# The routed experts' gate and up products, turned round: 32-place units and pieces of up to 384 tokens in place of tiles of 128 with the tokens standing

## The reference, cut to what matters

```python
xn = layernorm(x)                       # x: 8 x 1024 tokens of 512
s = recurrence(xn, W1, b1, W2, b2, init_h)       # gated scan over each sequence
# feed-forward part, T = 8192 tokens, E = 32 experts, H = 512, I = 1024
shared_out = (silu(xn @ sgw) * (xn @ suw)) @ sdw
topk_ids = argmax(xn @ gate_w)          # one expert for each token
xs = xn * sigmoid(max(xn @ gate_w))
g = grouped(xs sorted by expert, routed_gate_w)  # 512 -> 1024
u = grouped(xs sorted by expert, routed_up_w)    # 512 -> 1024
d = grouped(silu(g) * u, routed_down_w)          # 1024 -> 512
out = x + s * silu(shared_out + d in the tokens' order)
```

## Time and profile before

| | before |
|---|---|
| median of 3 runs | 4076.29 us (4075.59 to 4077.69) |
| the profiled execution's own time | 4077.65 us |
| its span in the trace | 4076.0 us |
| PE busy | 3984.7 us, 98% of the span |
| DVE busy, ACT busy | 1983.8 us (49%), 2003.6 us (49%) |
| POOL busy | 834.1 us (20%) |
| granted TensorE clock, mean | 0.991 |

### The profile page before, as it was taken

How to read it: one execution, slowest core, us unless ns; L and a number is a source line. 1 busy time by engine, 2 the same in 40 slices (tenths; PEclk the granted TensorE clock), 3 DMA queues, 4 the chain that set the end, 5 groups by cost and what they waited for, 6 DMA issues and landing times. The chain is left out here.

```text
span 4076.0 us, 51548 instructions
## 1 busy us (share of the span) xinstructions
PE 3984.7 (98%) x17849; PEld 3230.3 (79%) x17852; DVE 1983.8 (49%) x2711; ACT 2003.6 (49%) x2512; POOL 834.1 (20%) x927
## 2 busy tenths in 40 slices
PE   7999999999989999999999999799999999999998
PEld 6888888888867888888888888588888888888886
DVE  4232323233345555555555555455656556565564
ACT  3222222222247766766676666454545455554552
POOL 2011110101014100000000000043434434444443
PEclk9999999999989999999999999899999999999999
DMA  4122121212121000110000010455657557566562
GB/s 164 65 78 77 74 80 72 82 51 90 44 81 44 32 32 31 51 42 31 31 31 31 34 59 10 151 196 190 213 173 255 196 190 258 200 229 216 191 229 87
DMA packets 197850, 447.44 MB, mean 110 GB/s; under 512 B 19737, under 2 KB 36313, under 8 KB 193954
## 3 DMA queue, kind: packets, MB, share of 16 engines
q1 hardware_dynamic: 165170, 346.24, 24.0%
q0 software_dynamic: 32624, 100.47, 7.2%
HBM read 345.90 MB, written 104.68 MB: 111 GB/s over the span
## 5 line engine op out<-in xcount | busy, mean ns | idle before, releaser
L82 PE MATMUL gate<-xT,w_hi 128*128 128x512 f32 x1536 | 601.4, 392 | 1.1 <-DVE b2all L952 1.1
L83 PE MATMUL gate<-xT,w_hi 128*128 128x512 f32 x1536 | 601.4, 392 | 0.0
L84 PE MATMUL gate<-xT,w_lo 128*128 128x512 f32 x1536 | 599.6, 390 | 0.0
L1162 DVE TENSOR_TENSOR wlo<-raw,whi 128x2048 fp32r<-128x2048 f32 x192 | 438.7, 2285 | 83.5 <-ACT whi L1158 83.5
L1367 PE MATMUL tY<-whi,thT 128*128 128x512 f32 x1264 | 426.5, 408 | 0.0
L518 DVE TENSOR_TENSOR h_act<-h_act,psU 128x512 f32<-128x512 f32 x128 | 87.9, 687 | 685.8 <-PE psU L84 685.7
L1158 ACT ACTIVATE whi<-raw 128x2048 fp32r<-128x2048 f32 x192 | 367.3, 1913 | 42.1 <-DMA raw<-in_L_ffn_routed_gate_w 17.0
L82 PEld LDWEIGHTS gate<-xT,w_hi 128*128 128x128 f32 x1536 | 288.8, 188 | 66.2 <-DVE b2all L952 2.6
L84 PEld LDWEIGHTS gate<-xT,w_lo 128*128 128x128 f32 x1536 | 289.1, 188 | 62.1
L83 PEld LDWEIGHTS gate<-xT,w_hi 128*128 128x128 f32 x1536 | 288.8, 188 | 60.2
L966 DVE SCALAR_TENSOR_TENSOR log_f<-gate,b1s,log_f 128x512 f32<-128x512 f32 x128 | 96.2, 751 | 420.4 <-ACT log_f L893 420.4
(11 more groups left out here) (187 smaller groups left out, 8454.4 us busy)
## 6 DMA issues: line engine op xcount, KB each, us to landing
raw<-in_L_ffn_routed_gate_w SPq DMA_DIRECT2D x64, 1024.0 KB, 6.5
raw<-in_L_ffn_routed_up_w SPq DMA_DIRECT2D x64, 1024.0 KB, 6.3
raw<-in_L_ffn_routed_down_w SPq DMA_DIRECT2D x64, 1024.0 KB, 6.9
xT_dram<-xT SPq DMA_DIRECT2D x16, 2048.0 KB, 6.3
xT<-xT_dram SPq DMA_DIRECT2D x14, 2048.0 KB, 7.9
x_in<-in_L_attn_x SPq DMA_DIRECT2D x16, 1024.0 KB, 5.4
xs_dram<-x_in SPq DMA_DIRECT2D x16, 1024.0 KB, 4.4
ss_dram<-y_sb SPq DMA_DIRECT2D x64, 256.0 KB, 2.1
```

Source lines behind the costliest of these rows:

```text
L82: pe.matmul(out, w[0], x[0], start=start, stop=False)
L83: pe.matmul(out, w[0], x[1], start=False, stop=False)
L84: return pe.matmul(out, w[1], x[0], start=False, stop=stop)
L1162: dve.tensor_tensor(wlo[q][:], raw[q][:], whi[q][:], ALU.subtract).then_inc(wlo_done[q], 1)
```

## The change

The gate and up products are turned round. The standing operand is now a block of 128 weight columns, and the tokens of a *piece* of an expert stream past it. What comes out has the expert's inner channels on the partitions and the tokens along the free axis, which is the layout that `down` wants standing, so `turn_h` is gone. The work is in 8 blocks of 128 inner channels: each has 12 gate and 12 up matmuls of N columns. A piece has 256, 320 or 384 places (8, 10 or 12 units of 32), and each expert of this case is one piece. TensorE has the up part three times, once for each size, and branches to one of them (`by_size`). ScalarE and VectorE have one program, and work on 384 places whatever the piece has; PSUM is cleared at the start so that the places not computed hold numbers. `down` still works on 128 tokens at a time, two or three groups to a piece (`third`). `raw` is a ring of 3 tiles in place of 6, and each part is loaded by two DMAs; a part q below 4 now holds 256 columns of gate and the same of up. GpSimd gathers three groups for each piece, and scatters two or three.

In the diff below the first `piece` is ScalarE's and the second VectorE's. `silu(b)` writes `sg[b % 2]` from `psG[b % 2]`, `h_mul(b)` multiplies it by `psU[b % 2]` into `h[b % 2]`, `h_hi(b)` and `h_lo(b)` make of it the two parts in `hT`, all 384 places wide. There are two banks each for gate and up, so TensorE's gate products of a block wait for the silu of the block two before (`sg_done`), and its up products for the product of that block (`h_done`). There is one bank `tX`: `turn_x(p + 1, 1)` waits for `x_lo(p + 1, 0)`, and `turn_x(p + 1, 2)` for `x_lo(p + 1, 1)`. `total(g)` adds the shared part to tY of group g, `gated(g)` is its silu on ScalarE, `result(g)` multiplies by the recurrence's output and adds the residual.

In the first two sweeps the tables that describe the pieces are prepared: some ten more small VectorE operations in the sort, and in the first sequence of the recurrence a list of pieces (3 operations of 1 partition for each of 32 experts).

```diff
+UNIT = 32
+PIECE = 384
+SIZES = (8, 10, 12)
...
+                    if first and n >= NB:
+                        for e in range((n - NB) * z.E // NB, (n - NB + 1) * z.E // NB):
+                            list_expert(e)
...
-        raw = [k.sb(f"raw{q}", [P, 4, 512]) for q in range(PARTS)]
+        raw = [k.sb(f"raw{n}", [P, 4, 512]) for n in range(RING)]
...
+        def by_size(eng, n, body, sizes=SIZES):
+            if len(sizes) == 1:
+                return body(sizes[0])
+            half = len(sizes) // 2
+            with eng.If(n > sizes[half - 1]):
+                by_size(eng, n, body, sizes[half:])
+            with eng.Else():
+                by_size(eng, n, body, sizes[:half])
...
             def expert(e, split):
-                t0 = eng.value_load(starts[0:1, bass.ds(e, 1)], min_val=0, max_val=NS - 1)
-                t1 = eng.value_load(starts[0:1, bass.ds(e + 1, 1)], min_val=1, max_val=NS)
...
+                p = order(eng, FIRST_PIECE, e, 0, E + MOST)
+                full = order(eng, FULL, e, 0, MOST)
+                n = order(eng, LAST, e, LEAST, MOST_UNITS)
+                with eng.If(full > 0):
+                    with eng.Fori(0, MOST) as i:
+                        with eng.If(full > i):
+                            piece(p + i, e, MOST_UNITS, False)
+                piece(p + full, e, n, split)
...
+            def piece(p, e, n, split):
...
+                for b in range(NI):
+                    silu(b)
+                    h_hi(b)
+                    if b % 2 == 1 and b < NI - 1:
+                        hi(b // 2)
+                act.wait_ge(u_mm, p * NI + NI)
+                x_hi(p + 1, 0)
+                hi(NQ - 1)
+                for g in range(1, GROUPS):
+                    x_hi(p + 1, g)
                 hi(D0)
+                gated(0)
+                gated(1)
+                third(act, n, lambda: gated(2), lambda: act.sem_inc(zs_done[2], 1))
                 hi(D1)
...
+            def piece(p, e, n, split):
...
+                for b in range(NI):
+                    h_mul(b)
+                    h_lo(b)
+                    if b % 2 == 1 and b < NI - 1:
+                        lo(b // 2)
+                x_lo(p + 1, 0)
+                lo(NQ - 1)
+                for g in range(1, GROUPS):
+                    x_lo(p + 1, g)
+                total(0)
                 lo(D0)
+                result(0)
+                total(1)
+                result(1)
+                third(dve, n, last, absent)
                 lo(D1)
...
+            def up_part(p, e, n):
+                N = n * UNIT
+                def up(b, m, bank, done):
+                    q, cols = b // 2, slice(b % 2 * P, b % 2 * P + P)
                     for kb in range(KD):
+                        mm = matmul_pairs(pe, bank[b % 2][:, 0:N],
+                                          [pair(w[q][:])[:, m, kb, cols] for w in (whi, wlo)],
+                                          [xT[:, a, kb, 0:N] for a in range(2)], kb == 0, kb == KD - 1)
+                    mm.then_inc(done, 1)
+                for b in range(NI):
+                    if b % 2 == 0:
+                        pe.wait_ge(wlo_done[b // 2], e + 1)
+                    pe.wait_ge(sg_done, p * NI + b + 1)
+                    up(b, 0, psG, g_mm)
+                    pe.wait_ge(h_done, p * NI + b + 1)
+                    up(b, 1, psU, u_mm)
...
+                    by_size(pe, n, lambda size: up_part(p, e, size))
+                    turn_x(p + 1, 0)
+                    pe.wait_ge(wlo_done[D0], e + 1)
+                    pe.wait_ge(hlo, p * NI + KH)
+                    pe.wait_ge(z_done[0], p + 1)
+                    down(0, 0)
+                    turn_x(p + 1, 1)
+                    pe.wait_ge(z_done[1], p + 1)
+                    down(0, 1).then_inc(d0_mm, 1)
+                    turn_x(p + 1, 2)
+                    pe.wait_ge(z_done[2], p + 1)
+                    third(pe, n, lambda: down(0, 2).then_inc(d0_mm, 1), lambda: pe.sem_inc(d0_mm, 1))
+                    pe.wait_ge(wlo_done[D1], e + 1)
+                    pe.wait_ge(hlo, p * NI + NI)
+                    for g in range(2):
+                        down(1, g).then_inc(y_mm[g], 1)
+                    third(pe, n, lambda: down(1, 2).then_inc(y_mm[2], 1), lambda: pe.sem_inc(y_mm[2], 1))
```

More of the change, by code:

```diff
@@ new lines, in routed_sweep, with order, unit, third @@
+        out_stored = [k.sem(f"out_stored{g}") for g in range(GROUPS)]
+        block = ctx.enter_context(nc.Block())
+        def order(eng, what, e, least, most):
+            return eng.value_load(orders[0:1, what, bass.ds(e, 1)], min_val=least, max_val=most)
+        def unit(u):
+            return nc.s_assert_within(u, 0, NU, skip_runtime_bounds_check_because="the units of all experts are NU at most")
+        def third(eng, n, there, absent):
+            if isinstance(n, int):
+                return there() if n > 2 * STEP else absent()
+            with eng.If(n > 2 * STEP):
+                there()
+            with eng.Else():
+                absent()
@@ L1179, in tile @@
-            def tile(t, e, split):
-                pool.tensor_copy(at_this[:], gather_at[:, bass.ds(t, 1)]).then_inc(at_this_done, 1)
-                pool.wait_ge(at_this_done, t + 1)
+            pool.tensor_copy(at_x[:], gather_at[:, 0:WIDE]).then_inc(at_x_done, 1)
+            pool.wait_ge(at_x_done, 1)
+            for g in range(GROUPS):
+                fetch(xg[g][:], xs_dram, index(at_x, g), xg_loaded[g])
+            for g in range(GROUPS):
+                fetch(yo[g][:], x_rows, index(at_x, g), out_stored[g])
@@ L1210, in _ @@
+            with pool.Fori(0, E - 1) as e:
+                expert(e)
+            total, third, n = expert(E - 1)
+            for g in range(GROUPS):
+                pool.wait_ge(xg_loaded[g], (total + 1) * 16)
+            for g in range(2):
+                pool.wait_ge(out_stored[g], (total + 1) * 16)
             settle(pool, settled)
-            pool.wait_ge(out_stored, (total + 1) * 16)
+            with pool.If(n > 2 * STEP):
+                pool.wait_ge(out_stored[2], (third + 2) * 16)
+                settle(pool, settled)
@@ new lines, in down @@
+            def down(half, g):
+                q = D0 + half
+                for kb in range(KH):
+                    b = half * KH + kb
+                    for a, w in ((0, whi), (0, wlo), (1, whi)):
+                        mm = pe.matmul(psY[g][:], hT[:, a, b, g * P:(g + 1) * P], w[q][:, kb, :],
+                                       start=b == 0 and a == 0 and w is whi, stop=b == NI - 1 and a == 1)
+                return mm
+            total = order(pe, FIRST_PIECE, E - 1, 0, E + MOST) + order(pe, FULL, E - 1, 0, MOST) + 1
```

570 lines of the change are left out of this document (325 added, 245 removed).

## The result

| | before | changed |
|---|---|---|
| median | 4076.18 us (4075.59 to 4077.69, 4 runs) | 4126.65 us (4124.18 to 4131.06, 4 runs) |
| ratio, 95% interval | | 1.0124 [1.0107, 1.0142] |
| span of the profiled execution | 4076.0 us | 4124.8 us |
| PE busy | 3984.7 us, 98% | 3911.6 us, 95% |
| DVE busy, ACT busy | 1983.8 us, 2003.6 us | 2089.6 us, 2017.3 us |

The time lies inside the range of the prediction and on its slow side, 47 us above the forecast of no change. It is outside the forecast's own spread (4060 to 4110), that is, the spread without the rivals. TensorE did lose the work that the change takes from it (73 us less busy), and the kernel is slower all the same.

A forecast was written before the change was run, and what follows sets the result against it. TensorE bounds the kernel now; after the change, the ScalarE-VectorE chain bounds short pieces. Sweep 0, start +4, tail -1 make +3 on the profiled 4077.65; against medians 4079, stated as 4080 us, range 4045 to 4138.

The forecast's parts named there:

- TensorE's own work: TensorE's sum per piece without waits in the routed sweep: 36.4, 47.1 and 52.3 us for 256, 320 and 384 places.
- the fixed rest: Up part's matmuls: 0.0147 us beyond streaming stays the same at any width, giving 0.121 us at 256 columns.
- the branches and reads: At each piece's start TensorE idles for branches and table reads: 0.9 us, bounds 0.4 and 1.8.
- The chain: ScalarE-VectorE handoffs in 256-place pieces: 7.3 to first product, three pairs at 6.8, then 8.0 and 6.1; 41.8 us.
- the end 8.0: From block 6's product to the second token group's low part, with weight part 3's split between: 8.0 us.
- The clock: Rival: TensorE's clock falls in new pauses of 256-place pieces, up to 3.4 us each, 58 in all, 4138; chance 0.13.
- The start of the sweep: Ahead of the first silu, three token groups go through one bank, two more rounds at 2.0 each: 4 us later.
- The list: List of pieces made in the recurrence: hidden under TensorE, 0; as a rival it shows, up to +20, 4100, chance 0.04.
- The tail: At the kernel's end, the copy of the places already stands early, leaving only a wait: 1 us less.
- TensorE as the bound: Rival in the sweep: VectorE is not behind at the first product, so TensorE sets the pace: 3993 us; chance 0.08.
- Weight loads as the bound: Rival in the up part: narrow matmuls take the recorded load's 0.188 us, not 0.121: +230, 4310 us; chance 0.04.
- Far branches: Rival in TensorE's loop: some 64 size jumps each fetch code, 2.1 us, costing 60 to 134: 4140 to 4214; chance 0.05.

The follow-up runs named there:

- the three combined ones: Changed kernel with low parts later, list in two places, early loads, first weight splits first: 4010.09 us; plus three widths: 4012.87; instead plus two reads: 3985.70.

## Why the prediction was right and wrong

**TensorE's own work.** Right in the matmuls: 256 columns stand 0.120 apart (3530.28 to 3531.36 in nine steps), as the fixed rest had it (0.121). The page "TensorE: Matmul & The Clock Gate" of the Trainium skill ("What overlaps and what doesn't"), by which load and stream would take turns, does not describe this row. Wrong in the branches and reads, 0.9 a piece: the last tY matmul at 3527.18 and the first tG at 3527.41 stand 0.23 apart, one matmul's pitch. They cost nothing there, since the sequencer does them ahead, while matmuls are still queued. One of the two reads of that piece:

```profile
L1596 PEldq TENSOR_LOAD <-listed x1: 298/298/298, 3524.3 to 3524.3; - x1
```

The other is at 3525.0 and the last branch at 3525.8, 1.6 us before the first tG. TensorE's own time is 35.4 us for 256, 45.9 at most for 320 and 51.0 for 384, not 36.4, 47.1 and 52.3; the 0.1 to 0.4 beyond the 0.9 stay open.

**The chain.** This is the step that mattered, and it was right in its place and mechanism: pairs at 6.8 (measured 6.77 to 6.92), the end 8.0 (7.94), the rest 6.1 (6.15). The start was mis-sized: "a third table read beside them may show, so 7.3" should have been 0.7 for the read, with the branch behind it, and not 0.1. The 0.1 had no row behind it; the one row that I had was TensorE's 0.43 us for reads and branches together. VectorE starts its split at 3532.37 and its sequencer only then begins to read; reads and branch last 3.0 us, the split 2.3, and the 0.7 beyond it show. Without the third read the piece takes 41.8, the number forecast. With it, 15 pieces of 256 clear of the start took 0.8 more (12 us), and those of 320 took 47.9 for 47.3 (7 us in all); the two of 384 took 0.9 less each. (The prediction's words for a piece of 320 say 36 `down` matmuls behind the third group; its sum has 48, as the kernel does.)

**The clock.** The forecast had it at 1.00 throughout and made its fall a rival with up to 3.4 us a piece. It fell, 13 times for 3.4 us from the fourth piece on, in ten pieces of 256, and each of these took 0.6 more, whether it had one such stretch or two. Windows of two pieces of the changed kernel, without one and with two:

```profile
3390.15:3432.80 42.65, 36.78 (x254) 33.35 (x253) 27.82 (x32) 22.27 (x28) 18.54 (x14) 1.00 0.68 230
3432.80:3476.04 43.24, 38.94 (x254) 35.90 (x253) 27.81 (x32) 22.25 (x28) 18.65 (x14) 0.92 0.67 229
```

TensorE had pauses to give: most of what it loses at half clock, it would have waited. So the rival's event happened, with a tenth of its price, some 6 us (ten pieces at 43.2). With the low parts later, where TensorE waits for only 1.6 us of a piece (35.60 busy of 37.19), a drop costs 1.8 (38.98 and 37.19).

**The start of the sweep.** Predicted +4, measured +15.2; the step that failed is that three groups through one bank, 2.0 each, would set it. A group took 2.6 (ScalarE's copies start at 2627.80, 2630.40 and 2632.99), and the groups were not what ends last. The weight parts were, held back by SyncE's wait for three fetches behind a longer table, and I had not costed the wider table nor the four reads. That the loads are the cause rests on the kernels with the early loads: alone 44.9, within what the stretch varies by; in the three combined ones, which split the first weight parts ahead of the tokens as well, 41.6, 41.4 and 40.9, below every other kernel with the change. The two edits aren't told apart, and of the way back to 34.4 some 7 us stay.

**The list.** Predicted 0 with a rival at 0.04; measured 6.1. "VectorE follows at 763 of 1446 us" is an average; in the unit the gap of 2.4 us where the output sums still hide was asked for 3.0.

**The tail**: -1 predicted, -0.3 measured.

**The other rivals.** TensorE as the bound: not so here, but one change of order away, at 4019. Weight loads as the bound: no. Far branches: they cost, but only in the first three pieces. At the end of the second piece, ahead of the first one of 320 places, TensorE's sequencer spends 3.54 us on one branch of `by_size`, and TensorE stands still for 2.34 (the branch by line 1224; 70 ns is the other one):

```profile
L1224 PEldq COMPARE_BRANCH  x2: 70/1804/3537, 2735.4 to 2735.6; - x2
...
2739.35 0.41 PE L87 MATMUL tG<-txT,whi 128*128 128x320 f32 x1 [2.34 <-issue]
```

(PEldq is TensorE's sequencer.) The jump behind that up part, also of `by_size` (line 1226), takes 4.95 us at 2764.99, and that piece is 0.7 longer than later ones; the branch into the first up part of all, 6.56 us at 2635.38, lies ahead of the first silu. No other branch of TensorE from there to the end takes over 0.25 us, though pieces of the three sizes go on taking turns. In the two kernels with a single up part none takes over 0.34, and their second piece (46.03 and 45.63) is no longer than those behind it, where the changed kernel's took 45.1 and not 42.6. The queue of instructions in the sweep:

```profile
q8 instruction: 8, 0.13, 0.0%
```

All eight are in by 2780, and one is at 2736.5, within the branch of 3.54 us. That fits the mechanism of the page "Runtime: NRT & Kernel Launch" of the Trainium skill ("Instruction fetch mechanics"), a fetch before a branch to code that is not held can go on; which code is held no trace shows. So some 64 jumps at 2.1 us were priced, and three came, worth 3 us from the first silu on. (The 2.1 was taken from transfers of 256 KB, not from small ones.)

Added up, in the profiled execution: forecast +3, measured +48.8. The sweep's +27.8 is 12 (read) + 6 (clock) + 7 (pieces of 320) - 2 (of 384) + 5 (the first two pieces, 2.3 of it the far branch); 11 more at the start, 6 for the list, 1 for the tail.

That the time still lies in the range is in part luck. The range reached up to 4138 for the sake of the falling clock at 58 us. The clock took 6, and what filled the rest was the read, the start and the list, two of them terms that had next to nothing in the sum. What was no luck is the chain: its place, its pace of 6.8 and its piece of 41.8.

## What to carry to other kernels

Busy shares of 62% and 49% said that VectorE and ScalarE had room; the order in which each split passed from one to the other said that they had none. Before work is taken from the engine that is the bound, write down the chain of the others from handoff to handoff, and give two engines that alternate on long items one item of lag: here that was worth 108 us, more than twice the loss. Price bookkeeping (reads, branches) by whether the engine's queue is full at that point, and small added work by the gap it lands in, not by the engine's free share.

## What the runs showed that I had not expected

- Reading a number from a table costs 0 on TensorE with work queued, and takes 0.7 us on VectorE, where three of them and a branch outlast the split of 2.3 us that they run beside: one read less for each expert, on it and on ScalarE, was worth 24 to 26 us, of which 17 short pieces by 0.8 are 14; most of the rest is 0.5 to 0.8 in each piece of 320. (The edit takes a branch with the read.)
- Matmuls of 256 columns stand 0.120 apart, those of 384 0.174 (3424.82 to 3425.69 in five steps), with a load for each hidden.
- Three branches of TensorE, at the first uses of two of its three up parts, took its sequencer 3.5 to 6.6 us each; every later jump between the same programs took under 0.25. Behind the first silu they cost some 3 us in all.
- Half-clock stretches of 3.4 us came 13 times from the fourth piece on in a sweep with pauses of 1 to 3 us in TensorE's work, 3 times with the low parts later, and not once behind the second piece in the kernels with wide streams. I have not found what decides in which piece they come; that stays open.
